# One stacked tile for the unpaired half window of each head in a three-layer grouped convolution

## The reference, cut to what matters

```python
x = x + _L0_conv_ref(_gn(x), ...)              # experts
x = x + _L1_conv_ref(_gn(x), w3, w7, w15, mix) # and so L2, L3

outs = [_causal_dwconv(x_flat, w) for w in (w3, w7, w15)]   # 3, 7 and 15 taps
y = jnp.concatenate(outs, axis=1).reshape(b, h, 3 * d, l).transpose(0, 3, 1, 2)
return jnp.einsum('blhm,dm->blhd', y, w_mix)
```

## Time and profile before

| | us |
|---|---|
| median of three runs | 1045.34 |
| the three runs | 1043.8, 1045.34, 1047.53 |
| the profiled execution, its own time | 1041.55 |
| its span, first to last instruction | 1039.9 |
| TensorE busy | 1002.4 |
| VectorE busy | 490.9 |
| ScalarE busy | 321.2 |
| GpSimd busy | 182.5 |

### The profile page before, as it was taken

The page is one execution under the profiler, slowest core; times in us unless marked ns, Lnnn a source line. Parts: engine busy times, 40 slices in busy tenths (PEclk is TensorE's granted clock), DMA queues, the critical chain, the costliest instruction groups (busy, mean ns, idle before and its releaser), DMA issues.

```text
span 1039.9 us, 14304 instructions
## 1 busy us (share of the span) xinstructions
PE 1002.4 (96%) x5143; PEld 838.7 (81%) x5144; DVE 490.9 (47%) x659; ACT 321.2 (31%) x437; POOL 182.5 (18%) x227
## 2 busy tenths in 40 slices
PE   5989999999999999999999999968999999999998
PEld 4578888888888888888888888858878987898787
DVE  6763362164146145136155164156624894389211
ACT  2622341144144144144244144122501221122123
POOL 1011121121112112112111111111400123003200
PEclk9999999999999999999999999989999999999999
DMA  9575119926953995961994985981566456654657
GB/s 375 227 288 178 31 21 395 373 70 236 391 190 93 408 325 189 393 245 43 401 372 138 412 287 233 360 277 51 199 182 175 162 170 193 183 183 142 202 155 209
DMA packets 84864, 238.10 MB, mean 229 GB/s; under 512 B 8416, under 2 KB 50656, under 8 KB 69920
## 3 DMA queue, kind: packets, MB, share of 16 engines
q1 hardware_dynamic: 76608, 214.54, 55.4%
q0 software_dynamic: 8080, 23.07, 9.3%
q10 hardware_dynamic: 144, 0.07, 0.0%
HBM read 129.91 MB, written 111.94 MB: 233 GB/s over the span
## 4 chain that ended last, share of the span: by engine, by line
PE 73%; issue 10%; DVE 8%; DMA 4%; SPq 4%; ACT 2%; ACTq 0%; DVEq 0%; POOLq 0%
PE gate_ps L1003 13%; PE up_ps L1003 13%; PE y_ps L990 9%; PE head_ps L1525 8%; PE head_ps L1529 8%; PE head_ps L1526 8%; PE y_ps L993 4%; SPq L443 3%; PE hT_ps L1015 2%; DMA w_raw<-in_w13T 2%; PE xT_ps L980 1%; PE head_ps L1537 1%; PE head_ps L1535 1%; PE head_ps L1536 1%; DVE w_lo L821 1%
## 5 line engine op out<-in xcount | busy, mean ns | idle before, releaser
L1525 PE MATMUL head_ps<-split,ring 128*128 128x256 f32 (+1 forms) x525 | 181.5, 346 | 2.2 <-ACT split L1212 1.3
L1003 PE MATMUL gate_ps<-front 128*128 128x512 f32 x560 | 176.1, 396 | 1.8 <-DVE xT_lo L850 1.5
L1529 PE MATMUL head_ps<-split,ring 128*128 128x256 f32 (+1 forms) x525 | 177.3, 338 | 0.3 <-DVE split L1329 0.3
L1526 PE MATMUL head_ps<-split,ring 128*128 128x256 f32 (+1 forms) x525 | 176.5, 336 | 0.0
L1003 PE MATMUL up_ps<-front 128*128 128x512 f32 x560 | 172.7, 389 | 0.0
L865 DVE TENSOR_TENSOR hidden<-silu,up_ps 128x1024 f32<-128x1024 f32 x35 | 42.7, 1221 | 227.2 <-ACT silu L624 227.2
L1003 PEld LDWEIGHTS up_ps<-front 128*128 128x128 f32 x560 | 105.1, 188 | 22.2
L1003 PEld LDWEIGHTS gate_ps<-front 128*128 128x128 f32 x560 | 102.3, 188 | 22.4 <-DVE xT_lo L850 1.7
L624 ACT ACTIVATE silu<-gate_ps 128x1024 f32<-128x1024 f32 x35 | 35.9, 1027 | 266.0 <-PE up_ps L1003 266.0
L990 PE MATMUL y_ps<-w_hi,hT_hi 128*128 128x512 f32 x280 | 112.2, 401 | 1.2 <-ACT hT_hi L606 1.2
L1525 PEld LDWEIGHTS head_ps<-split,ring 128*128 128x128 f32 x525 | 99.7, 190 | 13.7 <-issue 2.1
(11 more groups left out here) (191 smaller groups left out, 1282.2 us busy)
## 6 DMA issues: line engine op xcount, KB each, us to landing
filters<-rows SPq DMA_DIRECT2D x56, 1568.0 KB
w_raw<-in_w13T SPq DMA_DIRECT2D x32, 1024.0 KB, 16.3
w_raw<-in_w2T SPq DMA_DIRECT2D x16, 1024.0 KB, 5.5
ring<-filters SPq DMA_DIRECT2D x15, 1024.0 KB, 6.3
ring<-filters SPq DMA_DIRECT2D x18, 640.0 KB, 4.7
ring<-filters SPq DMA_DIRECT2D x18, 512.0 KB, 4.2
ring<-filters SPq DMA_DIRECT2D x33, 256.0 KB, 3.4
ring<-filters SPq DMA_DIRECT2D x96, 64.0 KB, 4.8
```

Source lines behind the costliest of these rows:

```text
L1003: last = nc.tensor.matmul(o[:, n, :], a[:, k, :], b[:, k, t, n * 512:(n + 1) * 512], start=(k == 0 and a is xT_hi and b is w13_hi), stop=( ...
L1525: nc.tensor.matmul(place, kernel_hi, x_hi, start=(u == 0 and a == 0), stop=False)
L1526: nc.tensor.matmul(place, kernel_lo, x_hi, start=False, stop=False)
L1529: nc.tensor.matmul(place, kernel_hi, x_lo, start=False, stop=False)
```

## The change

For the unpaired unit of each head, the last window is no longer run in full by three matmuls. GpSimd stacks the high part of its 64 lags (partitions 64 to 127) on the low part (partitions 0 to 63) in a tile of the new tensor `single`, by two copies before each task (`tail`); the ring gets, for that head, the filter's high part twice, once in either half, and its low part. Two matmuls do the window: the high filter by the stacked tile gives high by high and high by low at once, the low filter by the same tile gives low by high (its upper half is zeros). Each head's filters now take one or two runs, the two shared halves and three more DMAs; with fewer runs these are 98 DMAs in a layer in place of 64. `shared` has five slots in place of six; GpSimd goes through the tasks in order. `between` has a further point u = 3, ahead of the shared window; some totals stand one unit later. The add of task 0 stands after piece 12, one piece sooner.

```diff
 
 def head_parts(h):
 
-    return [(s, j, windows(s) - (m in head_shared(h))) for m, (s, j) in enumerate(head_units(h))]
+    return [(s, j, windows(s) - 1) for s, j in head_units(h)]
+
+
+def head_single(h):
+
+    return next(m for m in range(3) if m not in head_shared(h))
 
 
 def head_tile(h):
...
 
 def head_windows(h):
 
-    return sum(n for _, _, n in head_parts(h)) + 1
+    return sum(n for _, _, n in head_parts(h)) + 2
 
 
 HEAD_ORDER = (11, 12, 6, 13, 14, 15, 10, 7, 8, 9, 0, 1, 2, 3, 4, 5)
...
             for j in range(GROUPS) for pair in (0, 1, None)}
 
 
-EARLY_AT = {PIECE_OF[12, None]: range(3), PIECE_OF[10, None]: range(3, EARLY)}
+EARLY_AT = {PIECE_OF[11, None]: range(1), PIECE_OF[12, None]: range(1, 3), PIECE_OF[10, None]: range(3, EARLY)}
 
 
 def last_use(l, i):
...
     _old = [(_layer, _head) for _layer, _head in HEAD_SEQUENCE[:_i]
             if RING_PLACE[_head] < _at + head_windows(_h) and _at < RING_PLACE[_head] + head_windows(_head)]
     RING_AFTER.append(max((_n + 1 for _n, (_layer, _head, _) in enumerate(TASKS) if (_layer, _head) in _old), default=None))
-    RING_COUNT.append((_l + 1) * (len(head_runs(_h)) + 2))
-
-TILE_SLOT = {1: 0, 6: 0, 2: 1, 4: 2, 5: 3, 7: 4, 0: 4, 3: 5}
-SLOTS = 6
+    RING_COUNT.append((_l + 1) * (len(head_runs(_h)) + 5))
+
+TILE_SLOT = {1: 0, 3: 0, 2: 1, 4: 2, 0: 2, 5: 3, 7: 4, 6: 4}
+SLOTS = 5
+SINGLES = 3
+SINGLE_SLOT = {h: i % SINGLES for i, h in enumerate(HEAD_ORDER)}
 SHARES = ((1, 0), (2, 0), (1, 1), (2, 1), (4, None), (5, None), (7, None), (3, None), (6, None), (0, None))
-SHARE_AFTER_PIECE = {5: (1,), 9: (2,), 11: (3,), 17: (4,), 18: (5,), 21: (6, 7, 8)}
-SHARE_AFTER_TASK = {9: (9,)}
-SHARE_AFTER_PLACE = {8: (9,)}
 SHARE_OF = {(t, pair): max(i for i, (tile, part) in enumerate(SHARES) if tile == t and same_batches(part, pair))
             for t in range(GROUPS // 2) for pair in (0, 1, None)}
 
 
+def share_first(i):
+
+    tile, pair = SHARES[i]
+    return next(n for n, (h, part) in enumerate(LAYER_ORDER) if head_tile(h) == tile and same_batches(part, pair))
+
+
+def single_free(n):
+
+    _, h, pair = TASKS[n]
+    return max((m + 1 for m, (_, head, part) in enumerate(TASKS[:n])
+                if SINGLE_SLOT[head] == SINGLE_SLOT[h] and same_batches(part, pair)), default=None)
+
+
 def slot_free(l, i):
 
     tile, pair = SHARES[i]
-    first = l * LAYER_TASKS + next(n for n, (h, part) in enumerate(LAYER_ORDER) if head_tile(h) == tile and same_batches(part, pair))
+    first = l * LAYER_TASKS + share_first(i)
     return max((n + 1 for n, (_, h, part) in enumerate(TASKS[:first])
                 if TILE_SLOT[head_tile(h)] == TILE_SLOT[tile] and same_batches(part, pair)), default=None)
 
...
         shared = sb("shared", [P, SLOTS, 2, BATCH, LEAD + P], f32r)
+        single = sb("single", [P, SINGLES, BATCH, LEAD + P], f32r)
...
+        single_ok = sem("single_ok")
...
                     at, width = (RING_PLACE[h] + taken) * 2 * P, count * P
                     sp.dma_start(ring[:, at:at + 2 * n * width].bitcast(f32).rearrange("p (a n) -> p a n", n=width),
                                  filter_rows[:, 2 * (l * GROUPS + j0):2 * (l * GROUPS + j0 + n), SCALE_AT[s]:SCALE_AT[s] + width]).then_inc(ring_in[h], 16)
-                at = (RING_PLACE[h] + head_windows(h) - 1) * 2 * P
+                at = (RING_PLACE[h] + head_windows(h) - 2) * 2 * P
                 for half, m in zip((1, 0), head_shared(h)):
                     s, j, count = head_parts(h)[m]
                     begin = SCALE_AT[s] + count * P
                     sp.dma_start(ring[half * P // 2:(half + 1) * P // 2, at:at + 2 * P].bitcast(f32).rearrange("p (a n) -> p a n", n=P),
                                  filter_rows[P // 2:P, 2 * (l * GROUPS + j):2 * (l * GROUPS + j + 1), begin:begin + P]).then_inc(ring_in[h], 16)
+                at += 2 * P
+                s, j, count = head_parts(h)[head_single(h)]
+                begin = SCALE_AT[s] + count * P
+                sp.dma_start(ring[:, at + P:at + 2 * P].bitcast(f32), filter_rows[:, 2 * (l * GROUPS + j) + 1, begin:begin + P]).then_inc(ring_in[h], 16)
+                for half in range(2):
+                    sp.dma_start(ring[half * P // 2:(half + 1) * P // 2, at:at + P].bitcast(f32),
+                                 filter_rows[P // 2:P, 2 * (l * GROUPS + j), begin:begin + P]).then_inc(ring_in[h], 16)
 
             sp.wait_ge(filters_out, FILTERS_FREE + 16 * QUARTERS * CHUNKS)
             sp.wait_ge(lasting.w2_ok, 2 * E)
...
                     nc.gpsimd.tensor_copy(shared[half * P // 2:(half + 1) * P // 2, slot, :, bs.start:bs.stop, LEAD:LEAD + P],
                                           split[P // 2:P, j, :, bs.start:bs.stop, LEAD:LEAD + P].bitcast(f32)).then_inc(shared_ok, 1)
 
+            def tail(n):
+                l, h, pair = TASKS[n]
+                bs, at = batches(pair), SINGLE_SLOT[h]
+                j = head_units(h)[head_single(h)][1]
+                piece = l * len(PIECES) + PIECE_OF[j, pair] + 1
+                pool.wait_ge(high_ok, piece)
+                if single_free(n) is not None:
+                    pool.wait_ge(head_done, single_free(n))
+                nc.gpsimd.tensor_copy(single[P // 2:P, at, bs.start:bs.stop, LEAD:LEAD + P],
+                                      split[P // 2:P, j, 0, bs.start:bs.stop, LEAD:LEAD + P].bitcast(f32)).then_inc(single_ok, 1)
+                pool.wait_ge(low_ok, piece)
+                nc.gpsimd.tensor_copy(single[0:P // 2, at, bs.start:bs.stop, LEAD:LEAD + P],
+                                      split[P // 2:P, j, 1, bs.start:bs.stop, LEAD:LEAD + P].bitcast(f32)).then_inc(single_ok, 1)
+
             for l in range(LAYERS):
-                for i in range(len(SHARES)):
-                    share(l, i)
+                for n in range(LAYER_TASKS):
+                    if n == 0:
+                        tail(l * LAYER_TASKS)
+                    for i in range(len(SHARES)):
+                        if share_first(i) == n:
+                            share(l, i)
+                    if n:
+                        tail(l * LAYER_TASKS + n)
 
         @block.scalar
         def _(act):
...
             nc.vector.memset(split[:, :, :, :, 0:LEAD].bitcast(f32), 0.0).then_inc(split_zeroed, 1)
             lane_centre(0)
             nc.vector.memset(shared[:, :, :, :, 0:LEAD].bitcast(f32), 0.0).then_inc(split_zeroed, 1)
+            nc.vector.memset(single[:, :, :, 0:LEAD].bitcast(f32), 0.0).then_inc(split_zeroed, 1)
             lane_sums(1)
             lane_centre(1)
             lane_scale(0)
...
                 l, h, pair = TASKS[n]
                 i = HEAD_SEQUENCE.index((l, h))
                 if n == 0:
-                    pe.wait_ge(split_zeroed, 2)
+                    pe.wait_ge(split_zeroed, 3)
                 pe.wait_ge(ring_in[h], 16 * RING_COUNT[i])
                 if n >= BANKS:
                     pe.wait_ge(summed, n - BANKS + 1)
...
                             pe.wait_ge(low_ok, piece)
                         nc.tensor.matmul(place, kernel_hi, x_lo, start=False, stop=False)
                     at += count
+                between(n, 3)
                 a = head_parts(h)[head_shared(h)[0]][2]
                 kernel_hi, kernel_lo = (ring[:, (2 * at + part) * P:(2 * at + part + 1) * P] for part in range(2))
                 x_hi, x_lo = (shared[:, TILE_SLOT[head_tile(h)], part, bs.start:bs.stop, LEAD - a:LEAD - a + P] for part in range(2))
                 pe.wait_ge(shared_ok, 2 * (l * len(SHARES) + SHARE_OF[head_tile(h), pair] + 1))
                 nc.tensor.matmul(place, kernel_hi, x_hi, start=False, stop=False)
                 nc.tensor.matmul(place, kernel_lo, x_hi, start=False, stop=False)
-                last = nc.tensor.matmul(place, kernel_hi, x_lo, start=False, stop=True)
+                nc.tensor.matmul(place, kernel_hi, x_lo, start=False, stop=False)
+                at += 1
+                a = head_parts(h)[head_single(h)][2]
+                kernel_hi, kernel_lo = (ring[:, (2 * at + part) * P:(2 * at + part + 1) * P] for part in range(2))
+                x_both = single[:, SINGLE_SLOT[h], bs.start:bs.stop, LEAD - a:LEAD - a + P]
+                pe.wait_ge(single_ok, 2 * (n + 1))
+                nc.tensor.matmul(place, kernel_hi, x_both, start=False, stop=False)
+                last = nc.tensor.matmul(place, kernel_lo, x_both, start=False, stop=True)
                 last.then_inc(head_done, 1)
 
             def between(n, u):
 
                 l, k = divmod(n, LAYER_TASKS)
-                if l == 0 and k == 0:
+                if l == 0 and k == 0 and u < 3:
                     turn(2 + u)
                     if u == 2:
                         turn(HALVES - 1)
...
                     lane_means(PAIR + 1)
                 if l == 0 and k == 2 and u == 2:
                     lane_deviations(1)
-                if l == 0 and 3 <= k < 7:
+                if l == 0 and 3 <= k < 7 and u < 3:
```

(14 more changed lines are left out.)

## The result

The changed kernel takes 1034.57 us (median of four runs, 1033.25 to 1035.45) beside 1045.21 for the kernel before in four runs: a ratio of 0.9901, with a 95% interval of 0.988 to 0.9922. That is 10.6 us less. The prediction said 1036.7.

The account below looks back on a forecast made before the run. TensorE is busy 96% of the span, VectorE nearly full at layer beginnings. Stages 1.3 + 2.3 - 0.5 + 2.3 + 0.2 + 3.0 give 8.6 us: 1041.55 becomes 1032.9, the median 1036.7; range 1032.5 to 1043.5.

Parts of the forecast that it names:

- full gain: Rival: copies fall between VectorE's operations, head 5's filters in time, no waits at task 6; 10.6 to 11.2 us gained; chance 0.16.
- The matmuls removed: Three matmuls per task become two: at most 11.2 us; 2.3 us from tasks 6 to 15 of each layer.
- First layer: Tasks 0 to 5: six matmuls less, some at the lower clock, and task 5's wait of 0.25 us gone; 1.3 us gained.
- The totals: Crossings between layers: totals one unit later meet VectorE's reductions, total 5's stall goes; about +0.6 us without other costs.
- Head 5's filters: End of a layer, task 18: filters land 13.5 to 14.5 us after task 12; wait of 0 to 0.9, taken as 0.4.
- The slower rival: SyncE's 34 more DMAs per layer crowd: wait from 0.55 us per issue, loss from 0.85; chance 0.06.
- Large heads' filters: Heads 11 to 15: landing set by bytes, which stay equal; 0.3 us added.
- The copies' cost on VectorE: Tasks 0 to 5 of layers 1 and 2: twelve small copies at 0.15 us each, 1.8 us, from 0 to 4.8.
- VectorE becomes the bound: Rival: each small copy costs VectorE its full 0.40 us, pieces 3 us later in two layers; gain 2.8 us; chance 0.18.
- Task 6: Layer 1: low part of piece 14 used at 845.0, 0.5 us later than now, TensorE waiting about 1 us for it.
- Crossing 2: From layer 1 into layer 2, up to task 6: filters of head 13 already ended the wait; 0.2 us gained.
- GpSimd's order: Rival: task 6's copies stand behind its shared ones, done 0.1 us late; at 2 us the gain is 4.6; chance 0.12.

Follow-up runs that it names:

- e2: Changed kernel with the moves left out (totals and the add of task 0 at their old places), stacked tile kept: 1038.49 us, ratio 0.993.
- e11: Changed kernel once more, no edit, on another chip than the first repeat: 1034.74 us, ratio 0.9913.
- e8: Kernel before with the moves alone (totals one unit later, add of task 0 after piece 12): 1043.36 us, ratio 0.9989.
- e4: Changed kernel with the copies to the stacked tile made in the first layer alone, result wrong in layers 1 and 2: 1033.98 us, ratio 0.9894.
- e6: Changed kernel with each of the two small GpSimd copies of every task made twice: 1042.86 us, ratio 0.9983.
- e5: Changed kernel with a head's five small DMAs on their own semaphore, waited for before the shared window: 1033.72 us, ratio 0.9895.
- e10: Changed kernel with small DMAs on their own semaphore, task 6's copies ahead of the shared tile's, add of task 2 after piece 14: 1033.15 us, ratio 0.9897.
- e3: Kernel before without one of three matmuls per shared window, result incomplete; no copies, new DMAs or moves: 1034.18 us, ratio 0.989.
- e9: Changed kernel with every small copy made twice and task 6's copies ahead of the shared tile's: 1038.06 us, ratio 0.9939.
- e1: Changed kernel once more, no edit: 1034.33 us, ratio 0.990.
- e7: Changed kernel with only the add of task 0 put back after piece 13, totals as changed: 1036.70 us, ratio 0.9923.

## Why the prediction was right, step by step

It was right in direction and in where the time comes from, and 2 us short in size: 8.6 us were forecast, the layers gave 10.1 and the medians 10.6. That is just above the upper edge of its own case (6.5 to 10), and by the medians it is the rival "full gain" (10.6 to 11.2). By its mechanism it is not: that rival had no waits at task 6 and +0.6 at each crossing, and TensorE waits there in both layers. The range of 1032.5 to 1043.5 was wide enough for either. Two terms were too dear, the waits at task 1 were missed, one crossing gained by a late landing that only the kernel before has, and the moves were undervalued. The two crossings hold 1.9 us of error in one direction; the other stages are within 0.2 us each.

**The matmuls removed: right.** Tasks 6 to 15 give 2.29 and 2.20 of the 2.3 forecast, and the last stage 2.84 of 3.0. Every stage without VectorE's pressure takes its matmuls' full time.

**First layer: not contradicted, and not shown finely.** 1.17 of 1.3. But the three executions of the changed program differ by 1.1 us here, as much as the term, so that the agreement is partly luck. Task 5's wait of 0.25 is gone, as forecast. The text took it that the long wait of task 2 puts the clock down; in one of the three executions it doesn't (last section).

**The totals: right, and more important than written.** Total 5 meets its reduction without a wait (817.32), and the low part of piece 0 is waited for (0.24 idle, as forecast at 0.1 to 0.3; 0.40 over a stream). What the text lacked is what they would cost if left where they were: e2 shows 4.3 us with the add. The prediction counted the moves as part of one walk through the crossing, and so never priced the two parts of the change against each other.

**Head 5's filters: the sum right, its parts off against each other.** SyncE's rows from head 3's first DMA to head 5's last two, first layer:

```profile
790.97 0.37 SPq L1161 DMA_DIRECT2D ring<-filters  x1
791.39 1.28 SPq L1167 DMA_DIRECT2D ring<-filters  x2
...
800.78 0.59 SPq L1172 DMA_DIRECT2D ring<-filters  x1
801.41 1.13 SPq L1174 DMA_DIRECT2D ring<-filters  x2
```

From 790.97 to the last issue at about 802.0 are 11.0 us for 18 issues, 0.61 each, where 9.9 to 10.8 was expected; the set is complete 2.3 us after the last issue, not 3.3. Together 13.5 us after task 12 is done, the lower end of the forecast 13.5 to 14.5. TensorE is there in the same moment (804.18 to 804.34 is 0.04 more than a stream). The wait of 0.4 that the sum took was 0.04, and 0.1 in layer 1; the largest in the other two executions of the program was 0.21. With the same DMAs e2 had 0.77 over a stream there once, where the set was complete only 3.1 us after its last issue, so that the forecast range of 0 to 0.9 is borne out and its middle is not. The slower rival wanted 0.55 us per issue for a wait and 0.85 for a loss; the issues cost 0.61, so it had passed the first of its own points, and only the quicker landing kept it away.

**Large heads' filters: a wait that was missed, behind which others stand.** I added 0.3 us and foresaw no wait at task 1. Head 12's set took 9.0 us from its first issue to the last landing in layer 1, where the kernel before took 7.5: with the same bytes, four issues became six, over 4.0 us instead of 2.3, and the set was complete only 5.7 after the last of them. TensorE waited 0.75 us at task 1, 0.9 over a stream. In layer 2 the set took 8.0 and the high part of the piece ended the wait.

But the filters cost nothing that a crossing shows. In e11, the same program, they were in time in layer 1 too (8.5 us), and the high part of the piece ended the wait after 0.33; crossing 1 is 41.30 there and 41.34 here. The waits that the sum lacked are those for the two parts of task 1's piece: in e11 they are 0.48 and 0.47 over a stream in layer 1, and 0.49 and 0.47 in layer 2. The kernel before has neither, because total 5 made TensorE late; e8, which has the old DMAs and the moves, has them (0.39 and 0.46).

**The copies' cost on VectorE: right in kind, a fifth too dear.** Beside copies of 0.48 us VectorE's operations of 0.42 take 0.62, 0.50 and 0.61; GpSimd and VectorE in the timelines of both:

```profile
813.66 0.48 POOL L1225 CAST single<-split 64x256 fp32r<-64x256 f32 x1 [8.80 <-ACT split L1258]
...
824.32 0.48 POOL L1225 CAST single<-split 64x256 fp32r<-64x256 f32 x1
824.86 0.47 POOL L1228 CAST single<-split 64x256 fp32r<-64x256 f32 x1
```

```profile
813.80 0.62 DVE L1375 TENSOR_TENSOR split<-scaled,split 128x256 fp32r<-128x256 f32 x1
...
824.57 0.50 DVE L1367 TENSOR_TENSOR scaled<-scaled,rstd_c 128x256 f32<-128x256 f32 x1
825.00 0.61 DVE L1365 TENSOR_TENSOR scaled<-stream,mean_c 128x256 f32<-128x256 f32 x1
```

Over twelve copies e4 gives 0.11 and 0.12 us each and e6, by doubling, 0.11 and 0.09, where 0.15 was taken; 1.1 to 1.5 us in place of 1.8 for each crossing. The line through its own two prices (0.35 at 64x512, 0.8 at 64x1024) comes to 0.125 at 64x256, not near 0 as the text has it, and that would have been the better number. Both engines give way, since the copy too lasts 0.47 where alone it lasts 0.39 to 0.40, the 0.40 of the line through the earlier trace rows, and 0.74 to 0.75 beside the operations of 512 columns, which go from 0.69 to between 0.77 and 0.88 (835.11 to 837.74). The low part of piece 14 came 0.6 and 0.8 us later after task 15 than before (41.35 and 41.49 for 40.71 and 40.68), where 1.6 was forecast. The rival "VectorE becomes the bound" at 0.40 each is excluded by these two runs.

The Trainium skill (page SBUF — State Buffer, "Who interferes with whom") has the two lock each other out for a whole instruction. These runs show a part at this size: 0.09 to 0.12 us for a 0.40 us copy, about a quarter, and in both directions. The larger copies come nearer to it: 0.8 us for one of 64x1024, which takes 1.04 alone.

**Task 6: right that something is waited for, wrong about what.** The text expected about 1 us in layer 1 for the low part of piece 14. TensorE waited 0.45 (0.61 over a stream) for head 13's filters; the low part was ready at 842.33, 0.24 us after that first matmul and in time for the third. e4 removes the copies and the wait for filters grows to 1.53; e5 and e10 take the small DMAs out of the wait, and the large one or the low part ends it. Filters and low part stand within about half a microsecond, and to take away one is worth nothing that a time shows.

**Crossing 2: the sign right, the size not.** 1.28 for 0.2. There the kernel before waited 0.78 (0.95 over a stream) for head 13's filters, which were complete 7.0 us after their last issue (6.9 in e8); in layer 1 of those two it is 5.4 and 5.5, and in e3 5.8 and 6.0. The changed kernel waits 0.34. Its two crossings are alike (41.34 and 41.27), while the kernel before's differ by 0.93, and e3 gains 1.49 in this crossing with the old DMAs. So what came back beyond the forecast is mostly that late landing. Why it was late wasn't tried; it was in the first layer too, 7.0 and 6.8, where nothing waited for it.

**GpSimd's order: the closest rival.** The prediction had task 6's copies done 0.1 us after TensorE wants them. They are done just before. GpSimd's rows, and TensorE's first matmul that reads them:

```profile
849.58 0.97 POOL L1225 CAST single<-split 64x512 fp32r<-64x512 f32 x1
850.61 0.61 POOL L1228 CAST single<-split 64x512 fp32r<-64x512 f32 x1
```

```profile
851.41 0.39 PE L1591 MATMUL head_ps<-single,ring 128*128 128x512 f32 x1
```

851.22 against 851.41: 0.2 us of room. e6 shows the price once it is used up, 1.9 us at each of two places, 1.2 in the first layer and 0.4 twice, and e9 that at task 6 the order is the cause.

## What to carry to other kernels

When matmuls are taken away, and what replaces them slows a second engine that is nearly full, look at once for what TensorE waits for next, and move that too: here the moves alone were worth 1.45 us in the crossings, and 3.8 beside the stacked tile. Where several arrivals end a wait within half a microsecond of each other, price them as one; an experiment that removes one of them will say that it costs nothing, and so will the next. And where a set of DMAs gets more issues for the same bytes, set the time from first issue to last landing against its first use, at every place where it is used, and then look at what stands behind it: head 12's grew from 7.4 to 7.6 us to between 8.0 and 9.0, only head 5's had been worked out, and where it was the last to arrive the parts of the piece came close behind.

## What the runs showed of the hardware that was not expected

The first six tasks of the layers take 36.3 to 37.4 us in three profiles of one program. The difference arises behind one wait: in task 2 TensorE stands idle for 1.47 to 1.48 us, for the statistics of the second pair. The stretch of eight us that ends with this wait and the four us behind it, first in the changed kernel's first execution, then in e11 (us; busy of PE, PEld, DVE, ACT, POOL; clock, DMA share, GB/s):

```profile
707.50:715.50 8.00, 6.53 (x56) 6.32 (x54) 6.17 (x16) 0.42 (x1) 2.88 (x6) 1.00 0.01 2
715.50:719.50 4.00, 4.00 (x23) 3.81 (x23) 1.82 (x5) 0.77 (x3) 0.00 (x0) 0.60 0.00 0
```

```profile
709.70:717.70 8.00, 6.52 (x55) 6.32 (x54) 6.17 (x16) 0.42 (x1) 2.89 (x6) 1.00 0.01 2
717.70:721.70 4.00, 3.23 (x26) 2.83 (x26) 2.73 (x7) 1.95 (x6) 0.00 (x0) 1.00 0.00 0
```

Up to the wait the two are alike. Behind it the granted clock is 0.60 in the mean of four us in the one (0.58 in e1), mostly its lower level, and full in the other, with the same program and the same wait. From the first matmul of the layers to the end of task 3 the one has taken 26.7 us and the other 25.6, and that 1.1 us stays. What decides it isn't shown. A change that is worth 1 us there can't be judged by one profile. The longer stages of e7 (39.26) and e9 (39.77) have the low clock too (0.57 and 0.59) and waits of their own: 0.76 and 0.98 us at the first low part of task 1, then 0.80 for the late add in e7 and 1.18 for the doubled copies at task 3 in e9.

DMAs that SyncE issues one after the other don't land in that order: in e10 head 13's large one, issued at 833.46, landed after 8.4 us, at 841.88, and ended TensorE's wait, while four fifths of the semaphore increments of the five small ones issued behind it had come by 841.0. Only e5 and e10 can show this, since the large DMA has a semaphore of its own there. In the other kernels all DMAs of a head count on one semaphore, and only the moment when the whole set has landed can be read: for head 13 in layer 1 that is 8.0 us after the first issue in the changed kernel, 9.2 in e5 and 9.6 in e10.
